# The second block-sparse layer moved into the mixer's block

## The reference, cut to what matters

```python
def block_sparse(x, weight, bias, centroids, assignments):      # x: 1024 x 512
    dots = softmax(x @ centroids.T / 0.1)                       # 64 clusters
    hits = dots > 0.01
    query_sel, cluster_sel = any(hits, axis=1), any(hits, axis=0)
    row_sel = cluster_sel[assignments]
    dense = x @ weight.T + bias
    return where(query_sel[:, None] & row_sel[None, :], dense, 0)
```

## Time and profile before

| | us |
|---|---|
| time, median of 3 runs (lowest, highest) | 1932.94 (1925.08, 1934.68) |
| the profiled execution | 1926.93 |
| its span, first to last instruction | 1925.2 |
| PE busy | 1814.7 (94%) |
| PEld busy (weight loads, beside PE) | 1449.0 (75%) |
| DVE busy | 1346.9 (70%) |
| ACT busy | 1169.4 (61%) |
| POOL busy | 1442.1 (75%) |

### The profile page before, as it was taken

One profiled execution on the slowest core, in us unless ns is written; L12 is line 12 of the kernel. 1 busy time (PEld: TensorE's weight loads), 2 busy tenths in 40 slices (PEclk: granted clock), 3 DMA queues, 4 the chain that ended last, 5 costly groups with the idle time before them and its releaser, 6 DMA issues. The chain is left out here.

```text
span 1925.2 us, 32304 instructions
## 1 busy us (share of the span) xinstructions
PE 1814.7 (94%) x10780; PEld 1449.0 (75%) x10780; DVE 1346.9 (70%) x1710; ACT 1169.4 (61%) x2114; POOL 1442.1 (75%) x1435
## 2 busy tenths in 40 slices
PE   6998896978999999999999999999999999999977
PEld 4776674667888888788788887887888788888755
DVE  4664564576776876787778767776876786768755
ACT  3222433367775766767577767675776676677733
POOL 4212334539997999699879978997999799879954
PEclk8997998989999999999999999999999999999988
DMA  3000001022231232223222223222232132222211
GB/s 110 1 1 23 2 2 56 11 73 98 86 104 59 89 97 88 79 77 94 73 77 94 99 68 99 78 93 74 77 101 98 62 99 77 88 77 86 85 33 45
DMA packets 107258, 136.40 MB, mean 71 GB/s; under 512 B 9026, under 2 KB 74690, under 8 KB 107076
## 3 DMA queue, kind: packets, MB, share of 16 engines
q1 hardware_dynamic: 106116, 134.02, 21.3%
q10 hardware_dynamic: 960, 0.05, 0.0%
HBM read 131.41 MB, written 2.62 MB: 70 GB/s over the span
## 5 line engine op out<-in xcount | busy, mean ns | idle before, releaser
L144 PE MATMUL ps<-mix_xnT_hi,mix_w_hi 128*128 128x512 f32 x1152 | 462.5, 401 | 9.5 <-DVE mix_bT L1823 9.5
L146 PE MATMUL ps<-mix_xnT_hi,mix_w_lo 128*128 128x512 f32 x1152 | 455.1, 395 | 0.0
L145 PE MATMUL ps<-mix_xnT_lo,mix_w_hi 128*128 128x512 f32 x1152 | 454.7, 395 | 0.0
L1823 DVE SCALAR_TENSOR_TENSOR mix_xT<-ps,mix_cur,mix_xT 128x510 f32<-128x510 f32 x378 | 279.2, 745 | 143.2 <-ACT mix_xT L1643 134.3
L1562 POOL TENSOR_SCALAR_AFFINE_SELECT mix_spread<-mix_spread 128x256 f32<-128x256 f32 x512 | 304.5, 630 | 0.0
L1843 DVE TENSOR_TENSOR mix_decay<-mix_decay,mix_cb 128x1536 f32<-128x1536 f32 x128 | 295.0, 2342 | 5.5 <-ACT mix_decay L1669 4.6
L1692 ACT ACTIVATE mix_g_hi<-mix_gated 128x512 fp32r<-128x512 f32 x128 | 81.0, 633 | 331.1 <-POOL mix_gated L1539 298.8
L144 PEld LDWEIGHTS ps<-mix_xnT_hi,mix_w_hi 128*128 128x128 f32 x1152 | 217.5, 189 | 58.1 <-issue 11.2
L146 PEld LDWEIGHTS ps<-mix_xnT_hi,mix_w_lo 128*128 128x128 f32 x1152 | 217.1, 188 | 50.8
L1667 ACT ACTIVATE mix_decay<-mix_spread,mix_cur_ncum 128x256 f32<-128x256 f32 x512 | 253.7, 496 | 1.6 <-issue 1.6
L145 PEld LDWEIGHTS ps<-mix_xnT_lo,mix_w_hi 128*128 128x128 f32 x1152 | 217.6, 189 | 47.0
(11 more groups left out here) (302 smaller groups left out, 3335.8 us busy)
## 6 DMA issues: line engine op xcount, KB each, us to landing
mix_spread<-cum_rows SPq DMA_DIRECT2D x128, 512.0 KB, 4.1
mix_w_raw<-in_w_in_stream SPq DMA_DIRECT2D x144, 256.0 KB, 4.2
mix_wo_raw<-in_w_out_T SPq DMA_DIRECT2D x64, 256.0 KB, 3.6
att_w_raw<-in_w_attn_T SPq DMA_DIRECT2D x12, 256.0 KB, 4.1
x<-in_x SPq DMA_DIRECT2D x8, 256.0 KB, 4.6
out_rows<-x SPq DMA_DIRECT2D x8, 256.0 KB, 2.0
att_wp_raw<-in_w_proj_T SPq DMA_DIRECT2D x4, 256.0 KB, 2.6
mix_decay<-in_w_ffn_T SPq DMA_DIRECT2D x1, 1024.0 KB, 5.9
```

What stands on the lines that cost most here:

```text
L144: pe.matmul(out, lh, rh, start=(k == 0), stop=False)
L145: pe.matmul(out, lh, rl, start=False, stop=False)
L146: last = pe.matmul(out, ll, rh, start=False, stop=(k == tiles - 1))
L1823: dve.scalar_tensor_tensor(out=d[:, :, shift:T], in0=src[:, :, 0:T - shift], scalar=w[:, MK - 1 - shift:MK - shift], in1=d[:, :, shift:T], ...
```

## The change

- `build_ffn` is gone, with its block, the barrier ahead of it and its buffers. `first_layer` becomes `layer_parts`, made twice: for the first layer and, with other banks and semaphores, for the last one at the end of the mixer's block. The centroids' parts, the ones and the bias rows and the one-hot matrix that the first layer made are kept and used again (`makes` is False for the last layer); the weights are loaded again (SP, in the last group at k = 4, into the two buffers of B and C) and split again (ScalarE and POOL at the tail's start).
- The sums of squares stand behind output rows 0 and 1 instead of 0 to 3. VectorE adds a tile to x as soon as its factor is there and computes its statistics at once; output rows 4 to 7 are read between these adds. TensorE turns tiles 0 and 1 ahead of output rows 6 and 7.
- In the last layer both cluster logits come after all turns; the dense rows 0 and 1 are done in halves of 7 and 6 matmuls between turns 3 to 6. Rows 2 and 3 stand ahead of the best values' transpose, row 4 ahead of the mask, rows 5 to 7 behind it.
- The bias is added by a matmul of 128 rows, of which all but two are zeros, in both layers. The last layer so has no bias work on ScalarE and POOL; POOL adds the even tiles to x and VectorE the odd ones, as in the first layer.
- The centroids are loaded twice, side by side, so the logits of the second half of the tiles come out on partitions 64 to 127, and four transposes of 128 x 128 take the place of eight of 64 x 64, in both layers.

The diff, cut to its core (the removed `build_ffn` and most of the placing of buffers are left out). Behind the buffers come, in this order, the pieces of SP, POOL, ScalarE, VectorE and TensorE; `row_of_x(t)` is called ahead of each tile's statistics:

```diff
-def first_layer(nc, sh, ins, m, ln):
+def layer_parts(nc, sh, ins, tag, m, ln, logit_banks, turn_bank, dense_banks):
...
+    def load_w(sp):
+        for part in range(2):
+            sp.dma_start(m.w_raw[part], ins["w_ffn_T"][part * 2 * P:(part + 1) * 2 * P, :].rearrange(
+                "(k p) n -> p k n", p=P)).then_inc(w_in, 16)
     def loads(sp):
-        sp.wait_ge(made, 1)
-        sp.dma_start(m.c_raw[:, :, 0:NCL], ins["centroids_T"]).then_inc(c_in, 16)
...
+        for half in range(2):
+            sp.dma_start(m.c_raw[:, :, half * NCL:(half + 1) * NCL], ins["centroids_T"]).then_inc(c_in, 16)
+        load_w(sp)
+        sp.wait_ge(made, 2)
+        sp.dma_start(m.bias[0:2, :], ins["ffn_bias"].partition_broadcast(2)).then_inc(bias_in, 16)
...
     def make(pool):
-        pool.memset(m.c_raw, 0.0).then_inc(made, 1)
+        pool.memset(m.bias, 0.0).then_inc(made, 1)
...
-        pool.memset(m.ones_raw, 1.0).then_inc(bias_done, 1)
+        pool.memset(m.ones_raw, 0.0).then_inc(bias_done, 1)
+        pool.wait_ge(bias_done, 1)
+        pool.memset(m.ones_raw[0:2, :], 1.0).then_inc(bias_done, 1)
...
     def turn_logits(pe):
         pe.wait_ge(logits_out, 2)
-        for t in range(NT):
-            last = pe.transpose(ps[:, 2, t * NCL:(t + 1) * NCL], m.logits_T[:, t * P:(t + 1) * P],
-                                sh.ident[0:NCL, 0:NCL])
+        for j in range(4):
+            last = pe.transpose(ps[:, turn_bank, j * P:(j + 1) * P], m.logits_T[:, j * P:(j + 1) * P], sh.ident[:, :])
...
-        m.bias_high, m.bias_parts = g_hi[0:2, 2, 0:C], g_hi[0:2, 2, C:2 * C]
-        m.ones_raw, m.two_ones = sb("ffn_ones", [2, P])[:, :], g_lo[0:2, 2, 0:P]
+        m.bias_high, m.bias_parts = g_hi[:, 3, 0:C], sb("ffn_bias_parts", [P, C], F32R)[:, :]
+        m.ones_raw, m.two_ones = u[:, 2, 0:P], sb("ffn_two_ones", [P, P], F32R)[:, :]
...
+                    if last and k == 4:
+                        sp.wait_ge(aux, n_aux(g, ("cb", B - 1)) + 1)
+                        last_layer.load_w(sp)
...
             add_square(MG - 1, PAIRS - 1)
-            group_rstd(MG - 1, TAIL + 4 + 2)
+            for k in range(2):
+                last_layer.w_low(pool, k)
+            group_rstd(MG - 1, TAIL + 4)
+            for k in range(2, KT):
+                last_layer.w_low(pool, k)
+            for t in range(NT):
+                lln.rstd_pool(pool, t)
+            for t in range(0, NT, 2):
+                last_layer.add_part(pool, t)
...
             square_pair(MG - 1, PAIRS - 1, False)
+            act.wait_ge(aux, n_aux(MG - 1, ("out", PAIRS - 1, 3)) + 1)
+            for k in range(KT):
+                last_layer.w_high(act, k)
+            act.wait_ge(summed, (PAIRS - 1) * MG)
+            last_layer.rows_act(act, False)
...
-            for t in range(4):
+            for t in range(2):
                 take_out(TAIL, t, t, False)
-            variance(TAIL + 4)
-            for t in range(4, NT):
+            variance(TAIL + 2)
+            for t in range(2, 4):
                 take_out(TAIL + 2, t, t, False)
-                if t == 4:
+
+            def row_of_x(t):
+                if 1 <= t <= 4:
+                    take_out(TAIL + 2, t + 3, t + 3, False)
+                if t == 0:
                     dve.wait_ge(rstd_done, MG)
-                add_row(t - 4)
-            dve.wait_ge(aux_free, TAIL + 2 + NT)
-            for t in range(4, NT):
-                add_row(t)
+                dve.wait_ge(aux_free, TAIL + 2 + max(t + 1, 4))
+                add_row(t).then_inc(x_added, 1)
+                dve.wait_ge(x_added, t + 1)
+
+            last_layer.rows_dve(dve, row_of_x)
+            last_layer.find_mask(dve)
+            for t in range(NT):
+                last_layer.take_dense(dve, t)
+                if t % 2:
+                    last_layer.add_part(dve, t)
...
+            last_rows(0)
+            last_rows(1)
+            sum_squares(MG - 1, TAIL + 2)
+            for t in range(2, 6):
+                last_rows(t)
+            lln.turn_pe(pe, 0)
+            last_rows(6)
+            lln.turn_pe(pe, 1)
+            last_rows(7)
+            pe.wait_ge(silu_g, 2 * PAIRS * MG)
+            pe.wait_ge(y_skip, 2 * PAIRS * MG)
+            lln.turn_pe(pe, 2)
+            for t in range(3, 7):
+                lln.turn_pe(pe, t)
+                last_layer.dense_rows(pe, (t - 3) // 2, False, *((0, 7) if t % 2 else (7, DENSE)))
+            lln.turn_pe(pe, 7)
+            last_layer.cluster_logits(pe, 0, False)
+            last_layer.cluster_logits(pe, 1, False)
+            pe.wait_ge(aux_free, TAIL + 2 + NT)
+            last_layer.turn_logits(pe)
+            last_layer.dense_rows(pe, 2, False)
+            last_layer.dense_rows(pe, 3, False)
+            last_layer.turn_best(pe)
+            last_layer.dense_rows(pe, 4, False)
+            last_layer.spread_mask(pe, False)
+            for t in range(5, NT):
+                last_layer.dense_rows(pe, t, False)
...
-        phases = ((build_attention, ()), (build_mixer, ()), (build_ffn, ("ffn2", out)))
+        phases = ((build_attention, ()), (build_mixer, (out,)))
```

More of the change, by code:

```diff
@@ L1213, in find_mask @@
         dve.wait_ge(mask_ps, 1)
-        dve.tensor_copy(m.mask, ps[:, 7, :]).then_inc(masked, 1)
+        dve.tensor_copy(m.mask, ps[:, ln.bank0 + 1, :]).then_inc(masked, 1)
         dve.wait_ge(masked, 1)
@@ L1220, in take_dense, with cluster_logits @@
             wait_x(dve, t - 4)
[L1221 removed]
+        dve.scalar_tensor_tensor(out=m.part[:, t % 4, :], in0=ps[:, dense_banks[t], :], scalar=m.row[:, 3, place(t):place(t) + 1],
                                  in1=m.mask, op0=ALU.mult, op1=ALU.mult).then_inc(dense_read, 1)
[L1225 removed]
+    def cluster_logits(pe, half, makes):
         pe.wait_ge(ln.s["lo"], 4 * half + 4)
[L1227 removed]
+        if half == 0 and makes:
             pe.wait_ge(c_done, 2)
         cols = slice(half * 512, (half + 1) * 512)
[L1230 removed]
+        three_pass(pe, ps[:, logit_banks[half], :], lambda k: (m.c_hi[:, k, :], m.c_lo[:, k, :]),
                    lambda k: (ln.hi[:, k, cols], ln.lo[:, k, cols])).then_inc(logits, 1)
@@ L1234, in turn_logits, with dense_rows @@
         pe.wait_ge(logits_out, 2)
[L1235 to L1237 removed]
+        for j in range(4):
+            last = pe.transpose(ps[:, turn_bank, j * P:(j + 1) * P], m.logits_T[:, j * P:(j + 1) * P], sh.ident[:, :])
         last.then_inc(turned, 1)
[L1240 to L1256 removed]
+    def dense_rows(pe, t, makes, first=0, end=DENSE):
+        bank, rows = ps[:, dense_banks[t], :], ln.place(t)
+        if first == 0:
+            if t == 0:
+                pe.wait_ge(w_lo_done, KT)
+                if makes:
+                    pe.wait_ge(bias_done, BIAS_STEPS)
+            if not makes:
+                pe.wait_ge(ln.s["lo"], t + 1)
+            if dense_banks[t] == turn_bank:
+                pe.wait_ge(sm, 2)
+            before = [u for u in range(t) if dense_banks[u] == dense_banks[t]]
+            if before:
+                pe.wait_ge(dense_read, before[-1] + 1)
+        for n in range(first, end):
+            if n == 0:
+                last = pe.matmul(bank, m.two_ones, m.bias_parts, start=True, stop=False)
+            else:
+                k, kind = (n - 1) // 3, (n - 1) % 3
+                last = pe.matmul(bank, (ln.lo if kind == 2 else ln.hi)[:, k, rows],
+                                 (m.w_lo if kind == 1 else m.w_hi)[:, k, :], start=False, stop=(n == DENSE - 1))
+        if end == DENSE:
+            last.then_inc(dense, 1)
@@ L1258, in turn_best, with spread_mask @@
     def turn_best(pe):
         pe.wait_ge(sm, 6)
-        pe.transpose(ps[0:NCL, 6, 0:P], m.best[:, :], sh.ident[:, :]).then_inc(best_T, 1)
-    def spread_mask(pe):
+        pe.transpose(ps[0:NCL, ln.bank0, 0:P], m.best[:, :], sh.ident[:, :]).then_inc(best_T, 1)
+    def spread_mask(pe, makes):
         pe.wait_ge(sm, SOFTMAX_STEPS)
-        pe.wait_ge(hot, 2)
-        pe.matmul(ps[:, 7, :], m.chosen[:, :], m.one_hot[:, :], start=True, stop=True).then_inc(mask_ps, 1)
+        if makes:
+            pe.wait_ge(hot, 2)
+        pe.matmul(ps[:, ln.bank0 + 1, :], m.chosen[:, :], m.one_hot[:, :], start=True, stop=True).then_inc(mask_ps, 1)
```

306 lines of the change are left out of this document (62 added, 244 removed).

## The result

The changed kernel took 1911.72 us in the median of 5 runs (1909.53 to 1914.12), the kernel before 1932.61 on the same chip in 5 runs: ratio 0.9911, 95% interval 0.9893 to 0.9929, so 13.7 to 20.7 us less. The forecast was 1916. Single runs of one program scatter here: over all sets of this study the kernel before was run 53 times (mean 1928.4, 1921.2 to 1934.7, standard deviation 3.9) and the changed one 11 times (mean 1912.3, deviation 2.5). Pooled over chips that is 16.2 us less, give or take 1.9. The forecast difference was 16.8. The median that it was taken from, 1932.94, lay high in that scatter, which is most of why the time came out under 1916.

The account below looks back on a forecast made before the run. The loop is TensorE-bound and unedited; gains lie before and behind it, in the first layer and a tail of single-step chains. Saving 14.0 + 2.8 = 16.8 us off the median 1932.94 gives 1916, range 1907 to 1924.

Parts of the forecast that it names:

- Part 2: First layer's dense rows: bias matmul on 128 rows instead of 2 saves 2.8 us, bounds 0 to 3.1.
- Part 1: Tail, from TensorE's restart behind the mixer's loop to the span's end: 14.0 us less, bounds 11 to 16.
- 0.3 for contention: Tail: VectorE's first add to x, beside POOL's third weight split, charged 0.3 us extra.
- The clock: Rival, tail: TensorE's clock falls between short work, costing about 3.5 us; time 1919.6, chance 0.24.
- signs of being wrong: Tail clock under 1.00 for over 4 us, first-layer dense row still 3.4, or VectorE idle between the statistics.
- no stall: Tail: output row 6 ready at 1865.6, VectorE wants it at 1865.8; tight, but VectorE does not wait.
- some 8: Last layer: its first mask row comes some 8 us earlier than before.
- Part 3: Last layer's weights: 1 MB more loaded in the loop's last group costs 0; without slack, up to 5.9 us.
- Half clock to the end: Rival, tail: TensorE stays at 1.2 GHz to the end; time 1940.7, chance 0.02.
- The first layer gave what it should: Rival, first layer: the edit saves nothing there, by another cause or VectorE's chain; time 1918.9, chance 0.12.
- VectorE and POOL shared badly: Rival, tail: 8 rows at 2.6 us instead of 2.2, costing 3 us; time 1919, chance 0.08.
- POOL has only small operations there: Tail: the argument against VectorE and POOL sharing badly, a rival of 3 us with chance 0.08.

Follow-up runs that it names:

- run 53: Not a run's label but a count: the kernel before, unedited, was run 53 times over all sets; mean 1928.4 us.
- fillers: Changed kernel plus 20 extra matmuls filling TensorE's idle times in the tail; median 1914.66 us, tail 63.6 us.
- two rows: Changed kernel with its bias matmul on 2 rows again in both layers; 1920.57 us, ratio 0.9951.
- two queues: Changed kernel with stores of odd rows issued from ScalarE's queue, even rows from SyncE's; 4.8 us from last add to end, no median given.
- halves earlier: Changed kernel with the half dense rows one turn earlier, no filler; 1914.06 us, tail 63.07 us.

## Why the prediction was right, and where it was not

*The sum.* Forecast 16.8 less, measured 16.2 (give or take 1.9) over all runs. That close a hit is partly luck: the edited stretches gave 12.1 to 13.3 in the profiles (9.4 or 10.6 in the tail, 2.7 in the first layer), and the rest stands in the loop, which I had at zero and for whose 4.7 us (mean 1471.9 over twelve profiles, 1476.6 over two) I have no shown cause, only a part of it by place: the stops among the output rows, 3.8 and 2.3 us without the change and none with it.

*Part 2, first layer, -2.8.* Right in size (2.7, and 2.6 alone in the kernel before) and in cause, which two experiments show. The first profile hid it: from the first statistics to the turned logits it took 1.7 longer. Over the 14 profiles this stretch was 25.6 four times, 26.2 once and 27.2 to 27.4 nine times, and it goes with the clock: the mean granted clock in it was 0.73 in the four, 0.67 in the one and 0.62 to 0.63 in the nine. At the same clock the kernels take the same time, so the 0.1 that I had for the logits' turn is not there. All nine have the change, the two without it are among the shorter five; whether the change makes the longer form likelier is not shown. One step of the reasoning was incomplete: I put the cost down to the short load alone, and the full load behind it waits as well.
The Trainium skill, TensorE: Matmul & The Clock Gate, section Step-by-step: what each phase is for, says that weight loads are pulled ahead of running matmuls, if row groups don't conflict or the load goes to the background buffer, and that the row count doesn't matter for their time. The trace agrees for the loads on 96 and 128 rows between matmuls on 128; those on 2 to 64 rows were not pulled ahead, which cost 0.35 us each.

*Part 1, tail, -14.0.* This is the mis-sized term: 9.4 in the first profile, 4.6 too much. Its pieces: the low clock 2.5 (66.1 against 63.6 with fillers); the last add to the span's end 1.3 (4.4 where I kept 3.1); the first add beside a split 0.5, the last beside POOL's add 0.3 (1.02 for 0.69); 0.3 for the start of VectorE's queue. I had charged 0.3 for contention, so 4.9 less 0.3. The clock was a rival at 3.5 and a chance of 0.24, and it came, in a shorter form: some 3 us of it behind the gap ahead of turn 0 and, in the first profile, some 3 more behind the gap ahead of turn 3, 6.8 in all. Two of the prediction's own signs of being wrong so came true in the first profile: a clock under 1.00 for more than 4 us, and VectorE idle between the statistics (1.59 ahead of row 6, where I had "no stall"). The path that I forecast for the tail failed there, and the loop made up for it. Its argument against, that gaps here are shorter than 3.47, failed too. Whether the low clock comes is different from execution to execution: of the eight profiles with an unfilled gap of 2.55 to 2.57 ahead of turn 0, five have it behind that gap and three (two rows, two queues, halves earlier) have not.
What held: sums behind row 1, VectorE's pitch (2.18 a row, I had 2.2), the softmax's first steps (4.87 from 1887.36 to 1892.23), TensorE about 1 us late at the best values, TensorE's end setting the last adds. The mask came 4.9 us earlier from the restart than before, not the "some 8".
The chain of waits shows that last part; the adds are at its end, with nothing but TensorE ahead:

```profile
1903.38 2.81 PE ps L1074 x12
1906.19 0.02 issue
1906.22 0.76 DVE mix_gated L1036
1906.98 0.02 issue
1907.00 1.02 DVE x L960
```

*Where the parts' worth lies.* Halves among the turns 4.9, sums behind two rows 1.6 to 2.8 (a delay of 1.0 that made two collisions of 0.5), 128 rows 5.0 in both layers together.

*Part 3, the load: 0.* Right. From the last sums in the loop to TensorE's restart it took 136.1 in both kernels. Over the 14 profiles it was 136.0 to 136.1 eight times and 137.6 to 137.8 six times, and of the two profiles without the load one is among the eight and one among the six.

*The other rivals.* Half clock to the end did not come near: 31 us from 1875 on had 1.00. The first layer gave what it should. VectorE and POOL shared badly where POOL had a full-width operation, at the first add to x and at VectorE's four last ones (1.22 to 1.23, the very last 1.02), of which the first and the very last are on the path. "POOL has only small operations there" overlooked its second pair of splits and its own adds. The end's clearing and the pair of stores stood in no rival: I had taken the old kernel's last 3.1 us over as they were, though the change merged two blocks and brought the last two rows together.

## What to carry over

When a change merges blocks, work out the end again: two stores 0.5 us apart and a longer clearing of semaphores cost 1.3 us behind the last add. Where two engines take turns in steps of 2 us, put real matmuls in the gaps (4.9 us here) or idle ones (1.3 to 2.5, seen in the tail alone and not in the medians), and keep full-width POOL work off the moment in which VectorE's chain starts. And where single runs scatter by 10 us, cut profiles at common events before crediting a stretch to an edit: here untouched code moved by up to 9 us.

## What the runs showed of the hardware

- A weight load on 2 to 64 rows was not pulled ahead of a running matmul on 128 rows (idle load queue 0.32 to 0.37 behind dense matmuls), nor was a load on 96 or 128 rows pulled ahead of a matmul on 2 or 64 (0.23 to 0.25). One short matmul among full ones cost 0.35 us in all. A load on 96 rows was pulled ahead of a matmul on 128.
- VectorE beside a full-width POOL operation took 1.27 and 1.77 for an add of 0.75, and 1.22 for one of 0.69; a small power on POOL beside VectorE's add took 1.08 for 0.58.
- Clearing semaphores took 5.4 ns each at the end of a block (24 more: 0.671 to 0.801; 32 more: 0.497 to 0.671).
- The last store of 256 KB landed in 2.0 us with 2.4 us since the store before it, in 2.45 with 1.2 and in 2.7 to 3.1 with 0.55.
- The same code had TensorE's low clock in one execution and not in another, worth 1.3 to 2.5 us in the tail and 1.7 in the first layer.
